# Perceiver block on one core: linear attention in 16 wide stages on row tiles, tail table moved forward

## What is computed

```python
x = x + xattn(layernorm(x), ctx)        # softmax attention of 256 queries over 4096 keys, then Wh, bh
x = x + linear_attn(layernorm(x))       # below
x = x + ffn(layernorm(x))               # silu(gate) * up, 768 wide, int weights scaled by 1/127

# linear_attn: q, k, v = split(x @ Wqkv + bqkv), per head, T = 256
xn   = x / max(norm(x), 1e-12)
arg  = clip((xn @ omega[r, h]) * sqrt(2 s_r) - s_r, -20, 20)      # r = 0, 1; 32 features each
feat = exp(arg) / sqrt(32) * sqrt(weight_r)                       # 64 features per head, for q and for k
out  = causal(qf @ kf.T) @ v / max(causal row sums, 1e-6)         # what the scan of the reference amounts to
out  = out @ Wout + bout
```

## Time and profile before

| | |
|---|---|
| median of 3 runs | 961.16 us (959.98 to 962.28) |
| the profiled execution | 961.61 us, its span 959.9 us |
| TensorE, matmul | busy 872.1 us (91%), 8803 instructions |
| TensorE, weight load | 608.0 us (63%) |
| VectorE | 443.8 us (46%) |
| ScalarE | 536.0 us (56%) |
| GpSimd | 68.3 us (7%) |
| DMA | 120.08 MB, mean 125 GB/s |
| chain that ended last | PE 73%, DVE 11%, issue 6%, ACT 5%, DVEq 2% |

### The profile page before, as it was taken

The page is one execution under the profiler, slowest core; times in us unless marked ns, Lnnn a source line. Parts: engine busy times, 40 slices in busy tenths (PEclk is TensorE's granted clock), DMA queues, the critical chain, the costliest instruction groups (busy, mean ns, idle before and its releaser), DMA issues.

```text
span 959.9 us, 20721 instructions
## 1 busy us (share of the span) xinstructions
PE 872.1 (91%) x8803; PEld 608.0 (63%) x8803; DVE 443.8 (46%) x847; ACT 536.0 (56%) x594; POOL 68.3 (7%) x124
## 2 busy tenths in 40 slices
PE   6799999999999988999999998999999999978676
PEld 5566666666566666666666665676666666656565
DVE  5522334554744345544743445535554444224553
ACT  2177777676565655656566555657566566840111
POOL 1033000000010000000011000000000000000120
PEclk9899999999999999999999999999999999999899
DMA  5666553566232333436233332345333331201000
GB/s 164 239 216 227 206 181 139 188 219 188 78 147 85 111 114 130 152 107 210 72 144 121 111 133 100 126 139 175 123 131 113 132 111 45 67 24 23 1 1 13
DMA packets 58736, 120.08 MB, mean 125 GB/s; under 512 B 21520, under 2 KB 29712, under 8 KB 55120
## 3 DMA queue, kind: packets, MB, share of 16 engines
q1 hardware_dynamic: 56848, 114.31, 34.6%
q0 software_dynamic: 1792, 4.40, 1.5%
HBM read 78.84 MB, written 37.75 MB: 121 GB/s over the span
## 4 chain that ended last, share of the span: by engine, by line
PE 73%; DVE 11%; issue 6%; ACT 5%; DVEq 2%; DMA 1%; POOL 1%; SPq 0%; ACTq 0%; POOLq 0%
PE ps_o L733 20%; PE ps_s L745 14%; PE ps_p L552 10%; PE ps_p L585 10%; ACT probs L1011 5%; PE ps_a L677 3%; PE ps_a L703 2%; PE ps_a L615 2%; PE ps_a L671 2%; PE ps_a L690 2%; DVE kparts L1050 1%; DVE kparts L1048 1%; PE ps_a L678 1%; DVE feat L1249 1%; PE ps_a L631 1%
## 5 line engine op out<-in xcount | busy, mean ns | idle before, releaser
L1011 ACT ACTIVATE probs<-ps_s 128x1024 f32<-128x1024 f32 x512 | 495.5, 1025 | 263.8 <-PE ps_s L745 236.1
L733 PE MATMUL ps_o<-probs,values 128*17 128x256 f32 x4096 | 252.0, 381 | 0.0
L745 PE MATMUL ps_s<-qstack,kstack 64*128 64x256 f32 x2048 | 201.4, 309 | 19.3 <-ACT probs L1011 18.5
L745 PEld LDWEIGHTS ps_s<-qstack,kstack 64*128 64x128 f32 x2048 | 140.7, 185 | 121.1 <-ACT probs L1011 65.1
L733 PEld LDWEIGHTS ps_o<-probs,values 128*17 128x17 f32 x4096 | 105.2, 97 | 93.1 <-issue 7.3
L1048 DVE TENSOR_SCALAR kparts<-ps_p,b_heads 128x512 fp32r<-128x512 f32 x64 | 48.0, 750 | 114.1 <-PE ps_p L552 114.0
L1065 DVE TENSOR_TENSOR values<-ps_p,bv_pair 128x512 f32<-128x512 f32 x64 | 44.2, 691 | 88.5 <-PE ps_p L585 88.5
L989 ACT ACTIVATE feat<-feat,node_neg 128x512 f32<-128x512 f32 x32 | 23.1, 722 | 105.4 <-DVE feat L1249 105.4
L585 PE MATMUL ps_p<-wv_hi,ctx_hi 128*128 128x256 f32 x256 | 78.6, 307 | 1.6 <-DVE wv_lo L1036 1.6
L585 PE MATMUL ps_p<-wv_hi,ctx_lo 128*128 128x256 f32 x256 | 72.3, 283 | 0.0
L585 PE MATMUL ps_p<-wv_lo,ctx_hi 128*128 128x256 f32 x256 | 72.3, 282 | 0.0
(11 more groups left out here) (213 smaller groups left out, 892.5 us busy)
## 6 DMA issues: line engine op xcount, KB each, us to landing
kstack<-kscr SPq DMA_DIRECT2D x96, 512.0 KB, 5.0
kscr<-kparts SPq DMA_DIRECT2D x64, 512.0 KB, 2.7
ctx_raw<-ctxT SPq DMA_DIRECT2D x32, 512.0 KB, 6.7
...
```

What stands on the lines that cost most here:

```text
L733: last = mm(ps_o[32 * j:32 * j + DH + 1, g * S:(g + 1) * S], values[par][:, i, head_of_step(g, j), :], prob[:, j * S:(j + 1) * S], start=b ...
L745: last = mm(ps_s[s % 2][:, j * S:(j + 1) * S], kstack[par][rows, u, i * P:(i + 1) * P], queries[rows, u, :], start=True, stop=True)
L1011: nc.scalar.activation(probs[n % AHEAD][:, :], ps_s[n % 2][:, :], ACT.Exp, scale=float(DH) ** -0.5).then_inc(fast["exp_done"], 1)
```

## The change

Everything below is in `AT`, `HEAD_AT`, `WARM`, the linear attention's stages and the order around them.

- The linear attention has 16 stages instead of 28. A feature stage covers two pairs of heads: `om_sb` holds each pair's omega in 32 rows, and four matmuls on two 32-row tiles write two banks. A product stage covers two heads: each head's 64 feature rows are their own 64-row tile, four matmuls write two banks. The masked copies are gone; one GpSimd instruction weights the key features of both pairs.
- These wide stages use `ps_p` and `ps_a` together (now one tensor `ps_pa`). So a wide stage waits for the evacuation of the last projection, and the next projection for that of the wide stage. Alone they rotate over three two-bank buffers.
- VectorE's clip and mask and ScalarE's exponential take twice the width, half as often.
- The value steps are split in every round that has a wide stage.
- The tables: `yT` from step 19 to 12, `feat0` 37 to 32, `pv3` 85 to 82, `down` 121 to 118, and what lies between; the head's layernorm from 94 to 86; the conversion of late weights from step 90 to 80 of batch 0.
- `norm1` stands ahead of `qkT0`; `warm` issues 32 matmuls ahead of `qkT0` (15 before) and none ahead of `qkT1` (11 before).

```diff
-BANKS_ALONE = 4
+BANKS_ALONE = 3
...
-SETUP_STEP = 5 * STEPS + 10
+SETUP_STEP = 5 * STEPS
...
-AT = {"o": 1, "oT0": 3, "oT1": 4, "yT": 19, "wh": 20, "ln1T": 24, "qk0": 25, "ss0": 25, "qk1": 26, "ss1": 26, "v": 28,
...
+AT = {"o": 1, "oT0": 3, "oT1": 4, "yT": 12, "wh": 13, "ln1T": 17, "qk0": 19, "ss0": 19, "qk1": 21, "ss1": 21, "v": 24,
+      "norm0": 24, "norm1": 25, "qkT0": 25, "qkT1": 28,
+      "feat0": 32, "feat1": 38, "A0": 42, "A1": 46, "feat2": 48, "pv0": 50, "A2": 54, "A3": 58, "pv1": 60, "feat3": 62,
+      "A4": 64, "A5": 70, "pv2": 72, "A6": 74, "A7": 78, "pv3": 82, "o2T0": 84, "o2T1": 85, "y2T": 88, "wout": 89,
...
-WARM = {"yT": 18, "ln1T": 10, "qkT0": 15, "qkT1": 11, "y2T": 3, "ln2T": 10, "gu0": 3, "down": 5}
+WARM = {"yT": 18, "ln1T": 10, "qkT0": 32, "y2T": 3, "ln2T": 10, "gu0": 3, "down": 5}
...
+WIDE = FEATS + [f"A{p}" for p in range(H // 2)]
...
             if not alone or name == "down":
-                return ps_a
-            k = c.bank(clock, name) % BANKS_ALONE
-            return ps_s[k // 2][:, k % 2 * 512:(k % 2 + 1) * 512]
+                return ps_pa[:, :] if name in WIDE else ps_a
+            bank = (ps_s[0], ps_s[1], ps_o)[c.bank(clock, name) % BANKS_ALONE]
+            return bank[:, :] if name in WIDE else bank[:, 0:512]
...
+                if wide_out[0]:
+                    pe.wait_ge(fast["operand"], wide_out[0])
+                unit_out[0] = (fast["k_out"], q * 2 + j + 1)
...
                 pe.wait_ge(c["operand"], c.ready(clock, name, BANKS_ALONE if alone else 1))
+                if name in WIDE and not alone:
+                    pe.wait_ge(*unit_out[0])
+                    wide_out[0] = c.at("operand", clock, name)
...
                     for i in range(2):
-                        last = mm(bank[:, i * S:(i + 1) * S], om_sb[:, n, :], qkT[:, 2 * i + n // 4, :],
-                                  start=True, stop=True)
+                        for e in range(2):
+                            at, pair = e * 512 + i * S, 2 * n + e
+                            rows32 = slice(pair % 4 * 32, pair % 4 * 32 + 32)
+                            last = mm(bank[:, at:at + S], om_sb[rows32, pair // 4, :], qkT[rows32, 2 * i + pair // 4, :],
+                                      start=True, stop=True, skip_group_check=True)
...
-                    mm(bank[:, 0:S], kfeat[:, p % 2, n % 2, 0:P], feat[:, p % 2, 0, :], start=True, stop=True)
-                    last = mm(bank[:, S:S + P], kfeat[:, p % 2, n % 2, P:S], feat[:, p % 2, 0, P:S],
-                              start=True, stop=True)
+                    for first, at in ((0, 0), (P, S)):
+                        for e in range(2):
+                            rows64 = slice(e * ROWS, (e + 1) * ROWS)
+                            last = mm(bank[:, e * 512 + at:e * 512 + at + S - first], kfeat[rows64, f % 2, n % 2, first:first + P],
+                                      feat[rows64, f % 2, n % 2, 0, first:S], start=True, stop=True, skip_group_check=True)
...
+                        halves = s == 0 or any(name in WIDE for t in range(QUAD)
+                                               for name, _ in stages_at(b, p * STEPS + s + t))
...
-                        if s == 0 and n:
+                        if halves and n:
...
-                for k in range(2):
-
-                    pool.tensor_tensor(kfeat[:, p % 2, k, :], feat[:, p % 2, 1, :],
-                                       half_mask[:, k:k + 1].to_broadcast([P, S]), ALU.mult
-                                       ).then_inc(c["kfeat"], 1)
...
+                pool.tensor_tensor(kfeat[:, f % 2, :, :], feat[:, f % 2, :, 1, :],
+                                   feat_weight[:, :].unsqueeze(2).to_broadcast([P, 2, S]), ALU.mult
+                                   ).then_inc(c["kfeat"], 1)
...
-                    last = v.tensor_tensor(amat[:, n % GH, :], bank[:, 0:3 * P], causal[:, :], ALU.mult)
+                    last = v.tensor_tensor(amat[:, n % 2 * 2:n % 2 * 2 + 2, :],
+                                           bank[:, :].rearrange("p (e k) -> p e k", e=2)[:, :, 0:3 * P],
+                                           causal[:, :].unsqueeze(1).to_broadcast([P, 2, 3 * P]), ALU.mult)
```

More of the change, by code:

```diff
@@ L71 @@
 HEAD_GENERAL = ["ln0", "ln0T", "q", "qcopy0", "fullmax", "maxT", "qcopy"]
-LINEAR = ["feat1", "A0", "A1", "feat2", "A2", "A3", "pv0", "feat3", "A4", "A5", "feat4", "A6", "A7", "pv1", "feat5",
-          "A8", "A9", "feat6", "A10", "A11", "pv2", "feat7", "A12", "A13", "A14", "A15", "pv3"]
-LINEAR_AT = [QUAD * quad + place for quad in range(10, 22)
-             for place in ((2, 3) if quad % QUAD == 0 else (0, 1, 2) if quad % QUAD == 3 else (0, 1))]
-AT = {"o": 1, "oT0": 3, "oT1": 4, "yT": 19, "wh": 20, "ln1T": 24, "qk0": 25, "ss0": 25, "qk1": 26, "ss1": 26, "v": 28,
-      "norm0": 34, "qkT0": 35, "norm1": 36, "qkT1": 36, "feat0": 37, **dict(zip(LINEAR, LINEAR_AT)),
-      "o2T0": 88, "o2T1": 89, "y2T": 91, "wout": 92, "ln2T": 96, "gu0": 99, "gate0": 100, "gu1": 101, "gate1": 104,
-      "gu2": 105, "gate2": 108, "gu3": 109, "gate3": 113, "gu4": 115, "gate4": 116, "gu5": 117, "gate5": 120,
-      "down": 121}
+AT = {"o": 1, "oT0": 3, "oT1": 4, "yT": 12, "wh": 13, "ln1T": 17, "qk0": 19, "ss0": 19, "qk1": 21, "ss1": 21, "v": 24,
[5 rows of a table added]
 TAIL = list(AT)
-HEAD_AT = {"ln0": 94, "ln0T": 102, "q": 106, "kbd": 110, "max0": 112, "max1": 114, "max2": 116, "max3": 118,
+HEAD_AT = {"ln0": 86, "ln0T": 102, "q": 106, "kbd": 110, "max0": 114, "max1": 115, "max2": 116, "max3": 117,
            "maxT": 120}
-WARM = {"yT": 18, "ln1T": 10, "qkT0": 15, "qkT1": 11, "y2T": 3, "ln2T": 10, "gu0": 3, "down": 5}
+WARM = {"yT": 18, "ln1T": 10, "qkT0": 32, "y2T": 3, "ln2T": 10, "gu0": 3, "down": 5}
 NORMALISED = TAIL.index("oT1") + 1
-FEATS = [f"feat{p}" for p in range(H // 2)]
+FEATS = [f"feat{f}" for f in range(G)]
+WIDE = FEATS + [f"A{p}" for p in range(H // 2)]
 GATES = [f"gu{k}" for k in range(HB)]
@@ L93 @@
 NEEDS = {"maxT": "max3", "oT0": "o", "oT1": "o", "qk1": "ln1T", "v": "ln1T", "qkT0": "norm0", "qkT1": "norm1",
-         **{n: "qkT1" for n in FEATS}, **{f"A{h}": "qkT1" for h in range(H)},
-         **{f"pv{g}": f"A{GH * g + GH - 1}" for g in range(G)}, "o2T0": "pv3", "o2T1": "pv3",
+         **{n: "qkT1" for n in FEATS}, **{f"A{p}": "qkT1" for p in range(H // 2)},
+         **{f"pv{g}": f"A{2 * g + 1}" for g in range(G)}, "o2T0": "pv3", "o2T1": "pv3",
          **{f"gu{k}": f"gate{k - 2}" if k >= 2 else "ln2T" for k in range(HB)},
@@ L123, in __init__ @@
             "powered": (["ln0"], ["wh", "wout"]),
-            "acted": ([], FEATS + GATES), "kfeat": ([], [f"A{h}" for h in range(H)]),
+            "acted": ([], FEATS + GATES), "kfeat": ([], FEATS),
         }
@@ L579, in project_values @@
                     pe.wait_ge(fast["k_out"], q * 2 + 2)
+                if wide_out[0]:
+                    pe.wait_ge(fast["operand"], wide_out[0])
+                unit_out[0] = (fast["v_ready"], q * PAIRS + pair + 1)
                 hi, lo = ctx_hi[q % 2], ctx_lo[q % 2]
@@ L836, in _ @@
                             fast_slot(b, p, s + t)
-                        for t in range(LAG if s == 0 else 0, QUAD):
+                        for t in range(LAG if halves else 0, QUAD):
                             fast_values(n - LAG + t)
@@ L1329, in setup_tail @@
                 v.tensor_scalar(clip_least[:, :], node[:, :], -20.0, None, ALU.add)
[L1330 to L1332 removed]
+                v.tensor_scalar(feat_weight[:, :], weight[:, :], 0.0, 1.0 / M, ALU.max, ALU.mult)
                 dve.wait_ge(setup_pow, 2)
@@ L1380, in _ @@
                 c = general
+                v.memset(ps_o[:, :], 0.0)
+                dve.drain()
                 dve.sem_inc(c["k_out"], 1)
```

53 lines of the change are left out of this document (25 added, 28 removed), and 2 rows, old and new, of the table AT.

## The result

| | before | after |
|---|---|---|
| median of the runs timed together | 960.57 us (959.50 to 962.28) | 915.47 us (911.31 to 916.26) |
| profiled execution (span) | 961.61 us (959.9) | 914.84 us (913.1) |

In the profiled execution after, TensorE's matmuls are busy 844.7 us (93% of the span), VectorE 432.7, ScalarE 532.0 and GpSimd 48.3 us.

The account below looks back on a forecast made before the run. TensorE's order was taken to set the loop's time, and chains across engines the lone tail's. From 961.6 us, 46.9 less in the loop and 11.7 in the lone tail gave 903, range 893 to 925.

Parts of the forecast that it names:

- If a pair runs side by side: Wide stages on TensorE: each then costs what a narrow one did, with half as many, 8.7 us less per tail.
- Rival (a): Wide stages: row tiles don't run side by side in float32, so TensorE does the old work; 933 us, chance 0.12.
- Rival (c): Loop: wide stages and projections wait openly for each other's bank evacuations, so it gets slower; 1003 us, chance 0.03.
- Rival (b): Loop: more waits than found, features holding up ScalarE and y late by 2; 915 to 920 us, chance 0.12.
- main case: Whole kernel: the forecast mechanism holds, 893 to 914 us for the bounds of the new durations; chance 0.73.
- W: Linear rounds of the loop: time of one wide stage, taken as 0.95 us for features and 0.66 for products.
- Rounds 0 to 7: Start of a batch, moved table: the tail and head cost 11.3 us where 10.0 stood, +1.3.
- 21 to 31: Last rounds of a batch, moved table: the tail and head cost 20.0 us for 24.5, -4.5.
- the placing of the warming matmuls: Lone tail: 32 ahead of qkT0, none ahead of qkT1, so features start 3.9 us earlier.
- The tail alone: Last batch's tail: features 3.9 us earlier and the linear part 7.8 less, together 11.7.
- VectorE mostly sets the pace: Lone tail's linear part, after the first product: VectorE work of 15.2 us, in a sum of 21.6 for 29.4.
- (d): Clock rival, lone tail: each stretch at half clock costs 1 to 2 us, moving the number, not its sign; no chance given.

Follow-up runs that it names:

- e2: Changed kernel with both matmuls of each wide pair on one row tile, so features and products come out different: 959.32 us, ratio 0.9954.
- e3: Changed kernel with value steps split only in a chunk's first round, as before: 931.64 us, ratio 0.9677.
- e14: Changed kernel with only the product pairs on one 64-row tile, features still side by side: 945.51 us, ratio 0.9801.
- e6: Kernel before with its narrow stages in the new table's places, warming and norm order as before: 959.59 us, ratio 0.9967.
- e4: Changed kernel with the old warming counts (15 ahead of qkT0, 11 ahead of qkT1) and norm1 behind qkT0 again: 918.57 us, ratio 0.956.
- e1: Changed kernel with more warming matmuls: 38 ahead of qkT0, 4 ahead of feat0, 12 ahead of A0: 912.94 us, ratio 0.9496.
- e7: Changed kernel with the next batch's first norm (ln0) back at place 94 instead of 86: 916.14 us, ratio 0.9517.
- e9: Changed kernel with ln1T, qkT0, ln0T and q moved, and 4 and 12 warm operations ahead of feat0 and A0: 906.29 us, ratio 0.9427.

## Why the prediction was right, and where it was off

**Right: what bounds the loop, and the wide stages.** "If a pair runs side by side" was the step on which most rested, and it holds in full float32 (e2: 0.86 and 0.62 a stage, 23.3 in the loop). Rival (a) is out. Rival (c) is out, but its wait is real as soon as the value steps are not split (e3). Rival (b) is out as a cause here: y came in time in all batches of the changed kernel's trace, though by little, as e3 and e14 show.

**Luck in the number.** 915.5 lies outside the main case's 893 to 914 and where (b) stood, 915 to 920. What put it there is not (b) but the two misses below, both in the same direction; the range held by the part that was kept for another mechanism.

**The term that was mis-sized in the loop: W.** Linear rounds cost 14.3 instead of 12.7. The wide product stages take 0.75 to 0.85 in the loop, 0.82 in the mean of a tail's eight, where 0.66 was taken, and the feature stage 1.06 for 0.95: 8 x 0.16 + 4 x 0.11 = 1.7. The 0.66 came from the earlier trace rows, a product stage that follows another product stage and is followed by a feature stage; in the loop each wide stage stands alone and is followed by value steps of another layout. The trace of before has narrow stages that scores of another layout follow:

```profile
272.85 0.59 PE L677 MATMUL ps_a<-feat,kfeat 128*128 128x256 f32 x2
...
273.59 0.74 PE L745 MATMUL ps_s<-qstack,kstack 64*128 64x256 f32 x8
...
278.93 1.02 PE L671 MATMUL ps_a<-qkT,om_sb 128*128 128x256 f32 x4
...
279.88 0.74 PE L745 MATMUL ps_s<-qstack,kstack 64*128 64x256 f32 x8
```

The product stage takes 0.74 there, the feature stage 0.95. So the neighbours account for half of the product's 0.16 and for nothing of the feature's 0.11. The rest comes with the wide form, and no run takes it apart. The linear rounds take 80.0 to 80.1 in all three batches, so the miss is 1.6 in each, 4.8 of the 5.3 us that the loop missed. Rounds 0 to 7 (11.3 for 11.3) and 21 to 31 (19.9 for 20.0) came out, though not each part: qkT0 waits 1.18, not 1.9. Two of the other terms were also shown apart: e6 holds the one for rounds 21 to 31 alone, e4 the placing of the warming matmuls.

**Right: batch 3 saves less.** 10.4 against 15.7 (12.5 against 17.2 forecast); the difference between the batches, 5.3, was forecast as 4.7.

**Wrong: "The tail alone", the step "VectorE mostly sets the pace: ... 21.6".** 26.7 came. The sum was made at the full clock, and (d) allowed 1 to 2 for each low stretch; one of nearly 14 us cost 3.9 (e1). The other 1.2 is in the pace from the first product on, at the full clock. VectorE does not set it alone: over e1's 23 us it is busy 14.9, and in the changed kernel it stands behind value stages, at 871.32, 876.80 and 880.64:

```profile
871.32 0.42 DVE L1272 COPY qk<-ps_s 128x256 f32<-128x256 f32 x1 [1.02 <-PE ps_s L701]
```

For these waits on TensorE the sum had nothing, except perhaps the last in its 1.5 at the end. The -3.9 ahead of the features came as -3.5 in this trace (-1.7 to -2.5 in e2, e3, e7 and e14, with low stretches of the clock elsewhere), and the stretch behind was 0.7 longer, so 5.5 stand for 11.7. The two misses, 5.3 and 6.2, with 0.25 by which batch 1 starts later (207.92 for 207.67), make up the 11.8 between the profiled 914.8 and the unrounded sum (961.6 - 46.9 - 11.7 = 903.0).

**Two tiles and four.** The Trainium skill's TensorEngine Tiling (Array Packing), Theoretical Speedup, gives up to 4x for a contraction of 32 and up to 2x for 64. Two tiles of each gave 1.92 / 1.06 = 1.8 and 1.47 / 0.85 = 1.7 with all switches, and four 32-row tiles 2 x 1.92 / 1.09 = 3.5 (e9): the trace agrees. Its section PSUM Bottleneck warns that evacuation may become the limit. No run shows VectorE full (47% of the span after); what e3 shows is a wait for one evacuation, 0.7 to 1.1 each time.
